# Row sums of a gated graph network, placed chunk by chunk among the other products of a step

## The chip, the cores and the metric

One Trainium2 chip, one core. The metric is the device time of one execution in microseconds; smaller is better. The kernel before ran in 6172.09 us (median of 3 runs, 6161.12 to 6196.0).

## The reference

A normalised input goes through a three-layer gated graph network (GGNN) and is added back. There are 12,500 nodes with 128 features, and 212,500 edges (src, dst), sorted by dst, with a self loop on each node.

```
h = relu(layernorm(x)) @ lin_w.T + lin_b
for i in range(3):
    m   = h @ weight[i]                          # messages, 12500 x 128
    agg = segment_sum(m[src], dst)               # per node, over its edges
    gi, gh = agg @ w_ih.T + b_ih, h @ w_hh.T + b_hh      # 3 gates each
    r, z = sigmoid(ir + hr), sigmoid(iz + hz)
    n    = tanh(in + r * hn)
    h    = (1 - z) * n + z * h
out = x + h
```

All of it is float32. Biases are small random values.

## The kernel before

**Data.** Messages are stored in DRAM as three bf16 pieces per row (384 values, 768 bytes) whose sum is the float32 value. Edges are handled in quads: 4 chunks (`QC`) of 128 edges. There are 416 quads, grouped in 13 superblocks of 32. Since edges are sorted by destination, the sums of one quad fall in a window of 36 nodes (`W`).

**Two ways to sum.** *Gathered quads*: GpSimd (POOL) fetches the 128 message rows of a chunk with one indirect DMA (L458); TensorE (PE) multiplies each of the 3 pieces by a 128 x 36 one-hot matrix of the edges' destinations (L699), 12 products a quad, accumulated in a PSUM window, and VectorE (DVE) adds the window to `aggT` at the quad's node offset (L1009). *Dense quads*, in layers 1 and 2 alone: the first 12 (`DQ`) quads of each superblock are replaced by a matrix of counts (source node x destination within the window), so that the sum is counts times all messages, which lie on chip (`pieces_region`). One dense block is 128 source nodes: 3 products of 128 x 432 (L730), accumulated over 98 blocks for each superblock in PSUM bank 6 or 7, then 12 adds on DVE (L1023).

**Layer 0** gathers all 416 quads and beside it makes the counts for layers 1 and 2: 156 dense quads x 7 rounds = 1092 counting rounds. DVE makes the one-hots of a round (4 instructions, L1089; every seventh round also 4 of L1078), PE multiplies them (4 products of 128 x 504, L712) into PSUM bank 6 or 7 alternately, ScalarE (ACT) copies the bank out (L581), and after seven rounds SP stores the counts (L405).

**Steps.** A step is two gathered quads: 8 gathers, 24 row products. Layer 0 has 208 steps, layers 1 and 2 have 130 each. `rounds_by(s)` and `blocks_by(s)` say how many rounds or dense blocks are to be done before step s: mostly six rounds a step (in steps 6 to 195), mostly ten dense blocks (30 products). A fixed table `TILES_AT` puts the update of each of 49 tiles of 256 nodes behind the step after which its sums are complete.

**Order on PE before.** Step s: wait for the rows, the one-hots of the step and the add of two steps ago; the 24 row products in one run, the last of which signals `s_sum`; the tile update if there is one (4 records for the messages of the tile before, 6 for the state, 6 for the gates; each float32 product leaves two records); then the step's rounds or dense blocks. Each round waits for its one-hots (`s_x`) and for ACT's copy of two rounds ago (`s_ev`).

**Who waits for the sum.** The gathered rows lie in a ring of four step slots (`RING`). POOL, before the gathers of step n, waits until PE has summed step n - 4 (`s_sum`). DVE's step s: add the sums of s (wait for `s_sum`), make half of the round one-hots of step s + 1, the tile update's part, the one-hots of the gathered rows of step s + 2 (L986), the other half of the round one-hots. ACT's step s: copy out half of the step's rounds, its part of the tile update (activations, table loads, stores of the state and the messages, the load of the next state tile), then the other half.

Of the kernel before, what the change touches and what calls it, by code (L numbers as in the profile page):

```python
# [5 lines left out]
P = 128  # L6
# [43 lines left out]
def gated_graph_layers(nc, x, src, dst, lin_wT, lin_b, weight, w_ihT, w_hhT, b_ih, b_hh, out, messages, states, counts):  # L50
# [75 lines left out]
    with ExitStack() as ctx:  # L126
# [192 lines left out]
        def window(n, q):  # L319
            return psum[:, 4 + n % 2, q * W:(q + 1) * W]  # L320
# [149 lines left out]
        def _(act):  # L470
# [117 lines left out]
            for s, n in each_step(0):  # L588
                r0, r2 = rounds_by(s), rounds_by(s + 1)
                r1_ = (r0 + r2) // 2  # L590
                for r in range(r0, r1_):
                    evacuate(r)
                for t in TILES_AT[0].get(s, ()):
                    with act.If(late < 1):
                        tile_update(0, t)
                    act.end_ifs()
                for r in range(r1_, r2):
                    evacuate(r)
            with act.If(late < 1):
# [15 lines left out]
        def _(pe):  # L615
# [74 lines left out]

            def sum_step(layer, s, n):
                pe.wait_ge(s_oh, n + 1)
                if n >= 2:
                    pe.wait_ge(s_add, 2 * (n - 1))
                pe.wait_ge(s_rows[n % RING], 16 * 2 * QC * (n // RING + 1))
                for h in range(2):
                    for c in range(QC):
                        for k in range(PIECES):
                            mm = nc.tensor.matmul(window(n, h), rows[:, n % RING, h * QC + c, k * P:(k + 1) * P],  # L699
                                                  onehot[:, n % 3, h * QC + c, :], start=(c == 0 and k == 0),  # L700
                                                  stop=(c == QC - 1 and k == PIECES - 1))
                mm.then_inc(s_sum, 1)

# [70 lines left out]
            for layer in range(LAYERS):  # L774
                extra_windows(layer)
                for s, n in each_step(layer):
                    sum_step(layer, s, n)
                    for t in TILES_AT[layer].get(s, ()):
                        with pe.If(late < 1):
                            tile_update(layer, t, s)  # L780
                        pe.end_ifs()
                    if layer == 0:
                        for r in range(rounds_by(s), rounds_by(s + 1)):
                            count_round(r)
                    else:
                        for d in range(blocks_by(s), blocks_by(s + 1)):
                            dense_block(layer, d)
                with pe.If(late < 1):
# [401 lines left out]
```

## Time and profile before

| | |
|---|---|
| median of 3 runs | 6172.09 us |
| profiled execution | 6174.11 us |
| its span | 6171.7 us |
| mean granted TensorE clock | 0.785 |
| instructions | 75641 |
| layer 0, 208 steps | 145 to 2853 us |
| layer 1, 130 steps | 2884 to 4506 us |
| layer 2, 130 steps | 4547 to 6149 us |

The span is from the first to the last instruction. PE is TensorE's products and PEld its weight loads, which run beside the products. A wait is put down to what released it; "issue" means that the profile shows nothing that the engine waited for, "remote" that the event that released it isn't in the records.

### The profile page before, as it was taken

To read this page: it belongs to the slowest core of one execution; us is meant where nothing else is said; L and a number is where in the kernel's file an instruction comes from. 1 tells how busy PE (TensorE), PEld (TensorE's weight loads), DVE (VectorE), ACT (ScalarE), POOL (GpSimd) and SP (SyncE) were. 2 spreads that over 40 slices of the span, in tenths; PEclk is the share of its full clock that TensorE was granted. 3 is DMA by queue.
4 is the path that set the end of the run, shared out by engine and by line. 5 is a ranking of instruction groups with operands and counts; after the bars stand their busy time and mean duration, and the time that the engine had idled before them with its cause. 6 is when DMAs were issued, how large, how long until landed. Compare 5 with 4: busy or idle time off the path is not lost.

```text
span 6171.7 us, 75641 instructions
## 1 busy us (share of the span) xinstructions
PE 3893.6 (63%) x25848; PEld 2077.0 (34%) x25849; DVE 2624.7 (43%) x11328; ACT 1090.7 (18%) x2007; POOL 4054.7 (66%) x3806
## 2 busy tenths in 40 slices
PE   4455655566555664652777777776647677677766
PEld 3222222222222222321344444343323344344433
DVE  6566766677675775841122222222211222222222
ACT  3233333333332332321000000010000000000000
POOL 5777777777777776775666666665636666666664
PEclk7677877787787787875888888888768888888888
DMA  6444444444444443454555555555545555555554
GB/s 207 130 125 123 129 125 123 127 131 124 126 126 115 132 129 106 139 160 111 172 176 163 165 177 169 170 177 166 164 148 169 166 176 172 168 170 166 170 162 117
DMA packets 662858, 921.28 MB, mean 149 GB/s; under 512 B 77112, under 2 KB 549304, under 8 KB 662456
## 3 DMA queue, kind: packets, MB, share of 16 engines
q1 hardware_dynamic: 394152, 483.63, 24.2%
q0 software_dynamic: 179712, 368.29, 21.9%
q10 hardware_dynamic: 88592, 64.25, 3.4%
q8 instruction: 221, 3.62, 0.2%
q14 instruction: 181, 1.48, 0.1%
HBM read 717.82 MB, written 198.05 MB: 148 GB/s over the span
## 4 chain that ended last, share of the span: by engine, by line
PE 33%; another core or an unknown queue 22%; issue 18%; DVE 14%; POOL 6%; ACT 3%; DMA 3%; DVEq 1%; ACTq 0%; POOLq 0%; SPq 0%
PE psum L730 16%; DVE pieces_region L1089 7%; PE psum L712 6%; POOL ring_region L458 6%; PE psum L699 3%; PE psum L688 3%; DVE onehot L986 3%; DMA temps<-states 2%; ACT pieces_region L581 1%; PE psum L659 1%; PE psum L661 1%; PE psum L660 1%; DVE aggT L1009 1%; DVEq L976 1%
## 5 line engine op out<-in xcount | busy, mean ns | idle before, releaser
L458 POOL DMA_INDIRECT ring_region<-messages,edge_src x3744 | 3994.1, 1067 | 2006.9 <-issue 1102.7
L712 PE MATMUL psum<-pieces_region,stage_region 128*128 128x504 bf16 x4368 | 1220.2, 432 | 928.6 <-issue 444.9
L730 PE MATMUL psum<-stage_region,pieces_region 128*128 128x432 f16 x7644 | 1648.5, 370 | 189.5 <-issue 188.3
L1009 DVE TENSOR_TENSOR aggT<-aggT,psum 128x36 f32 x936 | 178.8, 191 | 2611.7 <-remote 1994.6
L1089 DVE TENSOR_SCALAR pieces_region<-iota_round,stage_region 128x504 bf16<-128x504 f16 x4368 | 1281.5, 364 | 16.0 <-issue 15.0
L730 PEld LDWEIGHTS psum<-stage_region,pieces_region 128*128 128x128 bf16 x7644 | 761.8, 102 | 1009.1 <-issue 484.6
L699 PE MATMUL psum<-onehot,ring_region 128*128 128x36 bf16 x11232 | 476.4, 182 | 915.9 <-issue 688.6
L712 PEld LDWEIGHTS psum<-pieces_region,stage_region 128*128 128x128 bf16 x4368 | 416.9, 106 | 1633.2 <-issue 1146.9
L581 ACT CAST pieces_region<-psum 128x504 f16<-128x504 f32 x1092 | 621.5, 580 | 1733.5 <-remote 835.7
L699 PEld LDWEIGHTS psum<-onehot,ring_region 128*128 128x128 bf16 x11232 | 411.7, 99 | 1072.3 <-issue 984.8
L986 DVE TENSOR_SCALAR onehot<-iota_block,edge_rel 128x36 bf16<-128x36 bf16 x3744 | 570.5, 254 | 2.0 <-issue 1.9
L518 ACT ACTIVATE temps<-psum,small 128x256 f32<-128x256 f32 x147 | 69.8, 475 | 1813.0 <-DVE temps L1036 677.7
L688 PE MATMUL psum<-aggT,wih 128*128 128x256 f32 x882 | 270.5, 447 | 56.6 <-DVE aggT L1023 34.5
L540 ACT CAST pieces_out<-psum 128x256 bf16<-128x256 f32 x98 | 36.5, 372 | 1298.2 <-remote 911.9
L688 PEld LDWEIGHTS psum<-aggT,wih 128*128 128x128 f32 x882 | 203.0, 233 | 112.4 <-issue 75.0
L1049 DVE SCALAR_TENSOR_TENSOR temps<-psum,small,temps 128x256 f32<-128x256 f32 x147 | 71.0, 483 | 270.9 <-ACT temps L518 119.2
L1030 DVE TENSOR_TENSOR temps<-psum,pieces_out 128x256 f32<-128x256 f32 x98 | 41.3, 422 | 312.7 <-ACT pieces_out L540 201.0
L659 PE MATMUL psum<-temps,whh 128*128 128x256 f32 x294 | 116.8, 481 | 76.4 <-issue 43.3
L1023 DVE TENSOR_TENSOR aggT<-aggT,psum 128x36 f32 x312 | 60.3, 193 | 196.9 <-remote 87.8
L1078 DVE TENSOR_SCALAR stage_region<-iota_block,stage_region 128x128 bf16<-128x128 bf16 x624 | 121.7, 268 | 9.9 <-remote 7.8
L661 PE MATMUL psum<-temps,whh 128*128 128x256 f32 x294 | 114.3, 475 | 6.0 <-issue 5.8
L660 PE MATMUL psum<-temps,whh 128*128 128x256 f32 x294 | 113.7, 472 | 5.2 <-issue 4.8
(84 smaller groups left out, 1393.2 us busy)
## 6 DMA issues: line engine op xcount, KB each, us to landing
stage_region<-counts SPq DMA_DIRECT2D x364, 768.0 KB
counts<-pieces_region SPq DMA_DIRECT2D x156, 896.0 KB
ring_region<-messages,edge_src POOLq DMA_INDIRECT x3744
pieces_region<-messages SPq DMA_DIRECT2D x21, 1344.0 KB
temps<-states ACTq DMA_DIRECT2D x147, 128.0 KB
messages<-pieces_out ACTq DMA_DIRECT2D x98, 192.0 KB
states<-temps ACTq DMA_DIRECT2D x98, 128.0 KB
messages<-ring_region SPq DMA_DIRECT2D x25, 384.0 KB, 2.8
```

Source lines behind the costliest of these rows:

```text
L458: nc.gpsimd.indirect_dma_start(out=rows[:, n % RING, h * QC + c, :], out_offset=None, in_=messages[layer], in_offset=bass.IndirectOffsetOn ...
L581: nc.scalar.copy(ev[j % 2][:, 2 * i:2 * i + 2, 0:HB * W], psum[:, 6 + r % 2, 0:RW].rearrange("p (s w) -> p s w", w=HB * W)).then_inc(s_ev, 1)
L659: nc.tensor.matmul(GATE_R, whh[:, 0:P], state, start=True, stop=True)
L660: nc.tensor.matmul(GATE_Z, whh[:, P:2 * P], state, start=True, stop=True)
L661: nc.tensor.matmul(GATE_HN, whh[:, 2 * P:3 * P], state, start=True, stop=True).then_inc(s_hn, 1)
L688: nc.tensor.matmul(bank, wih[:, gate * P:(gate + 1) * P], nodes, start=alone, stop=True, skip_group_check=not alone).then_inc(s_gate, 1)
L699: mm = nc.tensor.matmul(window(n, h), rows[:, n % RING, h * QC + c, k * P:(k + 1) * P], onehot[:, n % 3, h * QC + c, :], start=(c == 0 and ...
L712: mm = nc.tensor.matmul(psum[:, 6 + r % 2, 0:RW], blocks_oh[j % 2][:, c, :], xs[r % XSLOTS][:, c, :], start=(c == 0), stop=(c == QC - 1))
L730: mm = nc.tensor.matmul(psum[:, 6 + kg % 2, 0:DQ * W], res[:, b, piece * P:(piece + 1) * P], stage[v % ABUF][:, :, cols], start=(b == 0 an ...
L986: made = nc.vector.tensor_scalar(onehot[:, n % 3, h * QC + c, :], iota_lo[:, 0:W], edge_rel[:, q * QC + c:q * QC + c + 1], None, ALU.is_equal)
L1009: nc.vector.tensor_tensor(cols, cols, window(n, h), ALU.add).then_inc(s_add, 1)
L1089: made = nc.vector.tensor_scalar(xs[r % XSLOTS][:, c, :], iota_hi[:], keys[:, j * QC + c:j * QC + c + 1], -float(RW * i), ALU.subtract, AL ...
```

## The change

On PE, a step's 24 row products are cut into eight chunks of three (one for each gathered chunk of 128 rows). After chunk i come the rounds, in layers 1 and 2 the dense blocks, from i/8 to (i + 1)/8 of the step's number. The last chunk signals `s_sum`; with six rounds, the last of them comes after it, with ten blocks the last two. The tile update follows the step's rounds or blocks, where it stood between the row products and them. ACT copies out all of a step's rounds ahead of its part of the tile update. Nothing changes on DVE, POOL and SP, and the number of instructions stays.

```diff
@@ ACT, layer 0
             for s, n in each_step(0):
-                r0, r2 = rounds_by(s), rounds_by(s + 1)
-                r1_ = (r0 + r2) // 2
-                for r in range(r0, r1_):
+                for r in range(rounds_by(s), rounds_by(s + 1)):
                     evacuate(r)
                 for t in TILES_AT[0].get(s, ()):
                     with act.If(late < 1):
                         tile_update(0, t)
                     act.end_ifs()
-                for r in range(r1_, r2):
-                    evacuate(r)
@@ PE
-            def sum_step(layer, s, n):
+            def rows_ready(n):
                 pe.wait_ge(s_oh, n + 1)
                 if n >= 2:
                     pe.wait_ge(s_add, 2 * (n - 1))
                 pe.wait_ge(s_rows[n % RING], 16 * 2 * QC * (n // RING + 1))
-                for h in range(2):
-                    for c in range(QC):
-                        for k in range(PIECES):
-                            mm = nc.tensor.matmul(window(n, h), rows[:, n % RING, h * QC + c, k * P:(k + 1) * P],
-                                                  onehot[:, n % 3, h * QC + c, :], start=(c == 0 and k == 0),
-                                                  stop=(c == QC - 1 and k == PIECES - 1))
-                mm.then_inc(s_sum, 1)
+
+            def sum_chunk(n, i):
+                h, c = i // QC, i % QC
+                for k in range(PIECES):
+                    mm = nc.tensor.matmul(window(n, h), rows[:, n % RING, i, k * P:(k + 1) * P],
+                                          onehot[:, n % 3, i, :], start=(c == 0 and k == 0),
+                                          stop=(c == QC - 1 and k == PIECES - 1))
+                if i == 2 * QC - 1:
+                    mm.then_inc(s_sum, 1)
@@ PE, the steps
                 for s, n in each_step(layer):
-                    sum_step(layer, s, n)
+                    rows_ready(n)
+                    if layer == 0:
+                        first, last = rounds_by(s), rounds_by(s + 1)
+                    else:
+                        first, last = blocks_by(s), blocks_by(s + 1)
+                    for i in range(2 * QC):
+                        sum_chunk(n, i)
+                        for j in range(first + (last - first) * i // (2 * QC),
+                                       first + (last - first) * (i + 1) // (2 * QC)):
+                            if layer == 0:
+                                count_round(j)
+                            else:
+                                dense_block(layer, j)
                     for t in TILES_AT[layer].get(s, ()):
                         with pe.If(late < 1):
                             tile_update(layer, t, s)
                         pe.end_ifs()
-                    if layer == 0:
-                        for r in range(rounds_by(s), rounds_by(s + 1)):
-                            count_round(r)
-                    else:
-                        for d in range(blocks_by(s), blocks_by(s + 1)):
-                            dense_block(layer, d)
```

## Rows read from the trace of the kernel before

**Rows 1.** The page, part 1: busy us, share of the span, instructions.

```profile
PE 3893.6 (63%) x25848; PEld 2077.0 (34%) x25849; DVE 2624.7 (43%) x11328; ACT 1090.7 (18%) x2007; POOL 4054.7 (66%) x3806
```

**Rows 2.** Windows, by layer: busy (records) of PE, PEld, DVE, ACT, POOL; granted clock; DMA.

```profile
145.00:2853.00 2708.00, 1523.80 (x10124) 723.15 (x10124) 1781.93 (x7384) 850.05 (x1469) 2000.36 (x1652) 0.75 0.46 129
2884.00:4506.00 1622.00, 1148.36 (x7690) 651.02 (x7690) 362.33 (x1762) 108.23 (x279) 982.54 (x1031) 0.81 0.55 170
4547.00:6149.00 1602.00, 1123.31 (x7598) 632.28 (x7598) 346.37 (x1717) 65.39 (x141) 979.80 (x1032) 0.82 0.52 163
```

**Rows 3.** Waits in layer 0: who, for whom, us in total, times, longest.

```profile
POOL ring_region L458 <- PE psum L699: 133.2, 21, 16.9
POOL ring_region L458 <- remote: 78.3, 23, 6.2
```

**Rows 4.** Waits in layer 1.

```profile
PEld psum L699 <- issue: 321.8, 293, 19.8
...
PEld psum L730 <- issue: 265.4, 564, 2.7
POOL ring_region L458 <- remote: 160.5, 58, 5.0
POOL ring_region L458 <- PE psum L699: 146.5, 40, 9.6
...
PE psum L699 <- DMA ring_region<-messages,edge_src: 20.8, 2, 19.6
...
PE psum L688 <- DVE aggT L1023: 14.9, 6, 4.1
```

**Rows 5.** Waits in layer 2.

```profile
POOL ring_region L458 <- remote: 182.2, 67, 4.1
POOL ring_region L458 <- PE psum L699: 116.6, 32, 7.1
```

**Rows 6.** Timeline, layer 1: start us, us, instruction, times [idle before].

```profile
4414.35 0.76 PE L699 MATMUL psum<-onehot,ring_region 128*128 128x36 bf16 x24
...
4414.57 1.20 DVE L986 TENSOR_SCALAR onehot<-iota_block,edge_rel 128x36 bf16<-128x36 bf16 x8
...
4414.96 5.64 PE L730 MATMUL psum<-stage_region,pieces_region 128*128 128x432 f16 x30
...
4416.06 0.94 POOL L458 DMA_INDIRECT ring_region<-messages,edge_src  x1 [0.30 <-issue]
...
4420.43 0.51 PE L699 MATMUL psum<-onehot,ring_region 128*128 128x36 bf16 x14
...
4430.51 1.25 PE L730 MATMUL psum<-stage_region,pieces_region 128*128 128x432 f16 x3 [1.59 <-issue]
```

**Rows 7.** Timeline, layer 0, a step with a tile update.

```profile
1116.20 1.46 PE L688 MATMUL psum<-aggT,wih 128*128 128x256 f32 x6
...
1119.80 2.78 PE L712 MATMUL psum<-pieces_region,stage_region 128*128 128x504 bf16 x12 [0.44 <-ACT pieces_region L581]
...
1120.11 0.50 DVE L1009 TENSOR_TENSOR aggT<-aggT,psum 128x36 f32 x2
...
1120.81 3.62 DVE L1089 TENSOR_SCALAR pieces_region<-iota_round,stage_region 128x504 bf16<-128x504 f16 x12 [0.20 <-PE psum L712]
...
1126.90 1.28 ACT L581 ACT_TABLE_LOAD   x1 [0.45 <-issue]
...
1128.92 1.84 PE L712 MATMUL psum<-pieces_region,stage_region 128*128 128x504 bf16 x4 [6.34 <-ACT pieces_region L581]
```

**Rows 8.** Timeline, layer 0, a sum whose signal comes late.

```profile
1410.01 0.93 PE L699 MATMUL psum<-onehot,ring_region 128*128 128x36 bf16 x24
...
1429.89 0.52 DVE L1009 TENSOR_TENSOR aggT<-aggT,psum 128x36 f32 x2 [20.76 <-remote]
...
1430.58 1.84 PE L712 MATMUL psum<-pieces_region,stage_region 128*128 128x504 bf16 x4 [16.16 <-ACT pieces_region L581]
...
1437.40 4.55 PE L712 MATMUL psum<-pieces_region,stage_region 128*128 128x504 bf16 x20
```

## The prediction

> **What bounds the kernel now.** I read the page first, then the table of windows by stage, the waits of each stage, and three short timelines.
>
> The page [rows 1] shows no engine near full: POOL 66%, PE 63%, DVE 43%. Such shares are averages over stages with different limits, so I cut the span at the layers [rows 2]. Layer 0 runs from 145 to 2853 us: 208 steps in 2708 us, 13.0 us a step. Layers 1 and 2 have 130 steps each, in 1622 and 1602 us, 12.5 and 12.3 us a step. The remaining 240 us are prologue, layer ends and the last tile; the change doesn't touch them.
>
> POOL first. A gather is 0.95 us and the 0.30 us after it [rows 6], so eight are 10.0 us. In layer 0 the records of POOL average 2000/1652 = 1.21 us [rows 2], 1.51 us with the 0.30: eight are 12.1 us. What POOL waits for beyond that is a ring slot, that is, PE's row sum of four steps ago: 133.2 + 78.3 = 211 us in layer 0 [rows 3], 146.5 + 160.5 = 307 us in layer 1 [rows 4], 116.6 + 182.2 = 299 us in layer 2 [rows 5] ("remote" has a missing semaphore record; the instruction waits for the same thing). Check: 208 x 12.1 + 211 = 2730 against 2708; 130 x 10.0 + 307 = 1607 against 1622. So layer 0 is set by POOL for 92% of its time, with PE late now and then; in layers 1 and 2 POOL is held up by PE in about 98 steps of 130.
>
> PE in layers 1 and 2. A step that runs freely takes 0.76 us for the 24 row products and 5.64 us for 30 dense ones [rows 6], 6.4 us, half of the 12.4. Yet the PE isn't waiting for rows (20.8 us in all of layer 1 [rows 4]). From 4420.4 on the same timeline shows why it is slow: 14 row products go at full speed, then the rest of that sum and the dense products after it come a few at a time, with idle gaps such as the 1.59 us ahead of three dense products at 4430.5, inside one accumulation, where the program has no wait. The waits put these gaps down to "issue": on the weight loads 321.8 us at the row products and 265.4 us at the dense ones in layer 1 [rows 4]. What holds instructions back I can't see, but their count fits: 2 x 7690/1622 = 9.48 loads and products per us in layer 1, 2 x 7598/1602 = 9.49 in layer 2, 2 x 10124/2708 = 7.5 in layer 0 [rows 2]. Two stretches with the same rate to 0.1%, made of quick 6.4 us steps and slow stretches, look like a limit on how many instructions PE gets through over time, not on array time.
>
> **The change part by part.** No instruction is added or removed, and the gathers, DMAs and evacuations are the same number. What moves is where the row sum ends, where the tile update stands, and ACT's order.
>
> 1. Layers 1 and 2, the sum's end. Each of the 8 chunks (3 products) is followed by an eighth of the step's 30 dense products. The sum, and so the signal that frees the ring slot and lets DVE add, now ends after 7/8 of the dense work: 0.875 x 5.64 = 4.9 us later at full clock. Behind it on POOL are that step's eight gathers. Does the PE then lack rows? A POOL that waits for a slot has three later steps already issued; three steps are at least 3 x 6.4 = 19 us of PE work, and the new gathers need 10.0 us plus their landing. With 4.9 us more, 19 - 10 - 4.9 leaves 4 us for it in the worst case, against 37 us at the average step. Cost 0; if the cover goes, up to 4.9 us at each of some 100 waiting steps a layer, 490 us a layer. That is the end above; I take 0, since the nearest row is the 20.8 us that PE waits for rows in layer 1 now. On DVE the one-hots of step n+2 are made behind the add of step n: add 0.50 [rows 7] and one-hots 1.20 [rows 6], needed a whole step (6.4 us) later. Hidden.
>
> 2. Layers 1 and 2, PE's time. Same instructions, same dense products; if the limit is their number per us, 0. This is my value. The end above it is the 606 us that POOL waits in both layers (the first rival); the end below is part 1's.
>
> 3. Layers 1 and 2, the tile update now comes behind the step's dense work. From one tile update to the next there is one step of dense work and one row sum, before and after. 0; the sums it needs are older then, which could give back a little of the 14.9 us that it waits for DVE's adds [rows 4].
>
> 4. Layer 0, the ring. The sum used to end 0.8 us into the step; now five of the (mostly) six counting rounds come before its last chunk. A round of 4 products is 4.55/5 = 0.91 us at the 2.4 GHz level and 1.84 us at 1.2 GHz [rows 8]: 4.6 to 9.2 us later. POOL waits 44 times in layer 0 [rows 3]. At each the slot now comes 4.6 to 9.2 us later, 202 to 405 us if nothing is given back. But a wait arises after PE was held up, mostly in the rounds, and PE then has three steps of rows to catch up on, so lost POOL time comes back in part where the next wait is shorter. I take a quarter of the middle, (202 + 405)/2/4 = 76 us; bounds 0 and 405.
>
> 5. Layer 0, DVE and PE in a ring of two. DVE makes the count one-hots of step s+1 after its add of step s. Before, the add needed only the quick sum; now it needs five rounds of the same step, which need DVE's previous step. So the shortest period is DVE's add, five rounds of one-hots, the gather one-hots, and then PE's last needed round, chunk and signal: 0.50 + 5 x 1.21 (a round: 3.62/3 [rows 7]) + 1.20 = 7.8, plus 0.91 to 1.84 for the round and some 0.6 us, an estimate, for the signal: 9.3 to 10.2 us. That is below POOL's 12.1, so in plain steps it costs nothing.
>
> In the 45 steps of layer 0 that have rounds and a tile update it isn't hidden. Today [rows 7]: adds at 1120.11, and the next ones only behind the sum that follows the round at 1128.92, so near 1132, 12 us later. PE does the tile products by 1117.7, five rounds by 1122.6, and then idles 6.34 us for ACT, which is in the tile update until 1126.9 and loads a table until 1128.2. After: the step began near 1117.7 - 3.9 (16 tile products at 1.46/6 = 0.24 us) - 0.8 = 1113.0. Sum and five rounds then end at 1113.0 + 0.8 + 5 x 1.0 = 1118.8 and the add starts near 1119.4; the last round and the tile products follow until 1123.7. PE's 6.34 us of idle goes. What is late next: ACT's part, which today takes some 7.7 us from its third copy (near 1120.5, the products are in the row of 1119.80) to 1128.2. The same from 1121 to 1123.7, when the gates come, ends at 1128.7 to 1131.4; DVE's part ends with it, less the table load of 1.28. Behind it stand the gather one-hots 1.2 and the fourth and fifth round 2.4, which the next step's sum now needs, and PE's round, chunk and signal 1.6: the next add comes at 1132.6 to 1135.3, 13.2 to 15.9 us behind the last one instead of 12. A plain step after it gives some 2 us back against POOL's 12.1. I take 1 us a tile step, 45 us; bounds -60 (some of the idle is gained) and 3.9 x 45 = 176, and 0.91 x 190 = 173 us more if the round that now lies between DVE's works shows in each of the 190 steps with rounds.
>
> 6. ACT's merged order and SP's stores of counts: each store waits for seven evacuations in a row that PE gates; they move by at most the half step and nothing waits for them but the second buffer after them. 0.
>
> The signal of a sum can be much later than its products: the products at 1410.01 are done in 0.93 us, DVE adds only at 1429.89, after 20.76 us of idle [rows 8]. The Trainium skill ("TensorE: Matmul & The Clock Gate", its table and "Back-to-back issue gap") has an instruction queue 64 deep on TensorE; the rows fit work that is queued and retired late, though none shows the queue. In the changed order such a delay would stand in DVE's loop too; that is in the upper end of part 5.
>
> **The sum.** Against the profiled execution, 6174.1 us around a span of 6171.7 (median of the runs 6172.1): 6174 + 76 + 45 - 15 (part 3) = 6280 us.
>
> **The rivals.** *Faster: the gaps come from the bursts.* In the timeline the slow stretch begins inside the 24 row products, which leave the queue at 0.76/24 = 32 ns each, against 188 ns for a dense one [rows 6]. If running out of fetched instructions there starts each slow stretch, spreading the burst prevents it, and POOL sets all layers: up to 606 us of its waits go, 5568 us. For it: the place where the gaps start. Against it: the equal rates in both layers, and gaps that go on through dense products. I price it at a quarter of the waits, 6174 - 150 = 6025.
> *No change:* PE's delay is absorbed, since POOL still sets layer 0 and instruction count layers 1 and 2: 6174. For it, POOL's 92%; against it, POOL's waits in layer 0 already today.
> *Much slower: the DVE-PE loop sets layer 0.* It decides if its period, 9.3 to 10.2 us plus the delayed signals, passes POOL's 12.1. At 14.5 us a step: 208 x 1.5 = 312, 6486 us.
> *The clock.* PE has 0.75 of full clock in layer 0, 0.81 and 0.82 after [rows 2]; a mean of 0.81 between the levels 0.5 and 1 means 38% of the time at 1.2 GHz. If spreading keeps it at 2.4 GHz, rounds gain 0.9 us each, but POOL's 12.1 us hides that: part of the second rival, or at best 1% in layer 0's waits.
> PE fell to 1.84 us a round after 16.16 us of idle and did 0.91 us rounds from 1437.4 on [rows 8]. The same page of the Trainium skill ("HAM oscillation") advises running products that belong together before the next wait, or the clock is lost; by it a change that puts the rounds' waits inside the sum goes towards "much slower", whose price from rows stands above. The trace agrees as far as the slow rounds after an idle stretch go.
>
> **How the numbers follow.** Forecast 0.46 (its own range 6215 to 6370), faster 0.22, no change 0.22, much slower 0.10. About 0.5%, 31 us, is what a measurement tells from no change. Faster by more than that 0.24 (the rival and an edge of "no change"), within 0.22, slower 0.54. For 8 in 10 the range reaches into both rivals: 6080 to 6450.
>
> **What would show it.** Layers 1 and 2 keep 12.3 to 12.5 us a step and 9.5 loads and products per us; layer 0 grows from 2708 to some 2820, with POOL's waits for PE well above 211 us and DVE's wait before the add longer. Wrong: if layers 1 and 2 shrink towards 10 us a step (the first rival); if layer 0 stays at 13.0 (parts 4 and 5 hidden); if PE waits for rows in layers 1 and 2 (part 1's cover was too thin).

## The result and the profile after

The change costs 0.6%: 6227.45 us (median of 20 runs, 6196.43 to 6252.46) against 6194.09 us for the kernel before beside it (20 runs, 6161.12 to 6233.08). The ratio is 1.0057, 95% interval 1.0038 to 1.0075. The forecast was 6280 us, 106 us above its profiled execution; the measured loss is some 35 us. The direction was right, the size three times too large, and the place wrong, as the profile shows: the direction was luck, since the two delays that the forecast added up in layer 0 came to nothing and the loss stands in a term that it put at 0.

The first part of the page of the changed kernel (busy us, share of the span, instructions):

```profile
PE 3946.1 (63%) x25848; PEld 2122.3 (34%) x25849; DVE 2619.8 (42%) x11328; ACT 1101.1 (18%) x2007; POOL 4058.4 (65%) x3806
```

Every count of instructions is that of [rows 1]. PE is busy 52.5 us longer and POOL 3.7 us. The windows of the changed kernel, one per layer (length, busy us and records of PE, PEld, DVE, ACT, POOL, granted clock, DMA share, GB/s), answer to [rows 2]:

```profile
145.00:2856.00 2711.00, 1528.85 (x10124) 794.26 (x10124) 1774.75 (x7384) 858.97 (x1469) 2010.95 (x1652) 0.81 0.46 128
2888.00:4524.00 1636.00, 1165.37 (x7690) 638.66 (x7689) 364.08 (x1761) 109.31 (x279) 977.76 (x1031) 0.82 0.54 168
4566.00:6194.00 1628.00, 1151.75 (x7595) 617.12 (x7593) 345.67 (x1716) 65.62 (x140) 976.81 (x1031) 0.81 0.52 160
```

The profiled execution took 6219.76 us, 46 us more than that of before. Layer 0, where the forecast put 121 us, went from 2708 to 2711 us, 13.0 us a step as before: the prediction's own sign that parts 4 and 5 are hidden. Layer 1 grew by 14 us and layer 2 by 26 us, and that is the loss. PE's granted clock in layer 0 rose from 0.75 to 0.81, and the layer is no shorter for it.

What POOL waited for in layer 0 of the changed kernel (us in total, times, longest), against [rows 3]:

```profile
POOL ring_region L458 <- PE psum L696: 133.5, 61, 11.9
POOL ring_region L458 <- remote: 78.2, 22, 6.5
```

211.7 us against 211.5, in 83 waits where there were 44. The waits of the changed kernel in layer 1, against [rows 4]:

```profile
PEld psum L728 <- issue: 368.2, 563, 2.7
...
PEld psum L696 <- issue: 295.4, 496, 2.7
...
PE psum L728 <- issue: 224.6, 292, 2.6
...
PE psum L696 <- issue: 192.0, 228, 2.3
POOL ring_region L458 <- PE psum L696: 172.6, 43, 8.6
```

The same view of the kernel before, its two rows for idle time ahead of the products themselves:

```profile
PE psum L699 <- issue: 284.0, 284, 2.7
...
PE psum L730 <- issue: 107.2, 168, 1.9
```

Ahead of the row and dense products, idle time of PE that the profile can't explain is 391 us in layer 1 before and 417 us after, and much of it moved from the row products to the dense ones. Ahead of the tile update's products it fell by as much, from 37 to 12 us. Its two largest rows before, then the largest one after:

```profile
PE psum L659 <- issue: 17.7, 8, 6.0
...
PE psum L672 <- issue: 12.0, 14, 2.5
```

```profile
PE psum L668 <- issue: 3.9, 8, 1.0
```

So PE's idle time doesn't hold the loss: all of it together is 1622 - 1148 = 474 us in layer 1 before and 1636 - 1165 = 471 us after. What grew is PE's busy time, by 17 us in layer 1 and 28 us in layer 2. The records explain how a hold-up can count as busy: each row product is recorded with 0.18 us (below), but in a run they overlap, so that 24 of them take 0.76 us. Standing apart they cover more time: the row products of layer 1 are busy for 147 us before and 271 us after, at the same number. I therefore count distances from the start of one PE product to the start of the next, leave out those where the second waited for something that the profile names, and call a distance of over 0.5 us held back. In layers 1 and 2 (e1 to e8 and f1 are runs described below):

| kernel | held back in layer 1, in layer 2 | time of these distances, both layers |
|---|---|---|
| before | 485, 493 | 1143 us |
| old order, ring of three (e6) | 479, 482 | 1099 us |
| changed | 531, 551 | 1228 us |
| changed, again (e5) | 543, 529 | 1218 us |
| changed, ring of three (e7) | 518, 536 | 1216 us |
| parts of the change on other chips (e1, f1) | 1 to 3 each | 2 us |

The three profiles of the new order have 1054 to 1082 such distances, the two of the old order 961 and 978. In the changed kernel they take 85 us more than before. The shorter distances behind row products take 25 us more too. About 70 us come back, at the tile update's products (347 to 303 us) and where a product waited for a cause that the profile names (91 to 64 us). What is left is the 40 us of the two layers.

The gaps themselves can be seen in the timeline of the changed kernel, layer 1, engine PE (start, length, instruction, times, idle before), where a free stretch ends and a held-back one begins:

```profile
4414.89 0.23 PE L696 MATMUL psum<-onehot,ring_region 128*128 128x36 bf16 x3
4414.97 0.71 PE L728 MATMUL psum<-stage_region,pieces_region 128*128 128x432 f16 x3
4415.51 0.36 PE L696 MATMUL psum<-onehot,ring_region 128*128 128x36 bf16 x3
4415.72 0.71 PE L728 MATMUL psum<-stage_region,pieces_region 128*128 128x432 f16 x3
4417.11 0.71 PE L728 MATMUL psum<-stage_region,pieces_region 128*128 128x432 f16 x3 [0.69 <-issue]
4417.85 0.18 PE L696 MATMUL psum<-onehot,ring_region 128*128 128x36 bf16 x1
4419.29 0.18 PE L696 MATMUL psum<-onehot,ring_region 128*128 128x36 bf16 x1 [1.26 <-issue]
```

Until 4416 a chunk and its share of dense products take 0.6 us. Then single products of one chunk, between which the program has no wait, stand 1.4 us apart. Cutting the burst of row products hasn't ended such stretches; there are more held-back products than before.

### The profile page after: what moved, and what is told of

Read it like the earlier page. It is cut to its first block, busy times and chain, and to the rows that moved or that the text cites. A ratio compares the mean times of both kernels' runs of the same rounds, so it can differ in the third digit from the quotient of the medians.

```text
span 6217.3 us, 75641 instructions
## 1 busy us (share of the span) xinstructions
PE 3946.1 (63%) x25848; PEld 2122.3 (34%) x25849; DVE 2619.8 (42%) x11328; ACT 1101.1 (18%) x2007; POOL 4058.4 (65%) x3806
## 4 chain that ended last, share of the span: by engine, by line
PE 38%; issue 21%; another core or an unknown queue 16%; DVE 12%; POOL 8%; ACT 2%; DMA 2%; DVEq 1%; ACTq 0%; POOLq 0%; SPq 0%
PE psum L728 21%; POOL ring_region L458 8%; PE psum L710 7%; DVE pieces_region L1093 6%; PE psum L696 3%; PE psum L684 2%; DVE onehot L990 2%; DMA temps<-states 1%; PE psum L655 1%; DVE aggT L1013 1%; PE psum L656 1%; PE psum L657 1%; DVE stage_region L1082 1%; ACT pieces_region L581 1%
## 5 line engine op out<-in xcount | busy, mean ns | idle before, releaser
L728 PE MATMUL psum<-stage_region,pieces_region 128*128 128x432 f16 x7644 | 1901.4, 381 | 453.8 <-issue 452.0
L710 PE MATMUL psum<-pieces_region,stage_region 128*128 128x504 bf16 x4368 | 1276.7, 425 | 915.1 <-issue 356.1
L696 PE MATMUL psum<-onehot,ring_region 128*128 128x36 bf16 x11232 | 866.4, 183 | 729.4 <-issue 485.3
L696 PEld LDWEIGHTS psum<-onehot,ring_region 128*128 128x128 bf16 x11232 | 799.3, 102 | 1520.8 <-issue 1017.0
L728 PEld LDWEIGHTS psum<-stage_region,pieces_region 128*128 128x128 bf16 x7644 | 631.8, 101 | 979.0 <-issue 743.9
L710 PEld LDWEIGHTS psum<-pieces_region,stage_region 128*128 128x128 bf16 x4368 | 368.8, 104 | 1306.3 <-issue 757.6
L518 ACT ACTIVATE temps<-psum,small 128x256 f32<-128x256 f32 x147 | 69.6, 474 | 1891.2 <-remote 1037.7
L684 PE MATMUL psum<-aggT,wih 128*128 128x256 f32 x882 | 236.2, 405 | 25.8 <-DVE aggT L1027 16.3
L684 PEld LDWEIGHTS psum<-aggT,wih 128*128 128x128 f32 x882 | 181.3, 207 | 62.0 <-issue 34.0
L655 PE MATMUL psum<-temps,whh 128*128 128x256 f32 x294 | 106.5, 443 | 52.3 <-DMA temps<-states 28.4
L656 PE MATMUL psum<-temps,whh 128*128 128x256 f32 x294 | 101.6, 430 | 4.0 <-issue 4.0
L657 PE MATMUL psum<-temps,whh 128*128 128x256 f32 x294 | 99.2, 421 | 2.9 <-issue 2.8
L520 ACT ACTIVATE temps<-psum,small 128x256 f32<-128x256 f32 x147 | 69.4, 472 | 103.2 <-remote 49.1
```

The costliest lines, as they stand in the source:

```text
L655: nc.tensor.matmul(GATE_R, whh[:, 0:P], state, start=True, stop=True)
L656: nc.tensor.matmul(GATE_Z, whh[:, P:2 * P], state, start=True, stop=True)
L684: nc.tensor.matmul(bank, wih[:, gate * P:(gate + 1) * P], nodes, start=alone, stop=True, skip_group_check=not alone).then_inc(s_gate, 1)
L696: mm = nc.tensor.matmul(window(n, h), rows[:, n % RING, i, k * P:(k + 1) * P], onehot[:, n % 3, i, :], start=(c == 0 and k == 0), stop=(c ...
L710: mm = nc.tensor.matmul(psum[:, 6 + r % 2, 0:RW], blocks_oh[j % 2][:, c, :], xs[r % XSLOTS][:, c, :], start=(c == 0), stop=(c == QC - 1))
L728: mm = nc.tensor.matmul(psum[:, 6 + kg % 2, 0:DQ * W], res[:, b, piece * P:(piece + 1) * P], stage[v % ABUF][:, :, cols], start=(b == 0 an ...
```

## Experiments

One thing must be known to read the numbers. The kernel before took about 6190 us in the runs of the result above and on the chip of e5 to e8, and about 5380 us on four other chips (e1 to e4, f, g and h, with 5385, 5373, 5383 and 5378 us). Each experiment is compared with the kernel before on its own chip. I say "slower kind" and "faster kind" of chip below; whether the difference belongs to the chip itself or to its condition in that hour no run shows. Several expectations name the other kind of chip than the one that the run then got; what that means for each is said beside its result.

**e5: the change as it is.** No edit.

> The whole change, unaltered, on the chip where the kernel before takes 5385 us and PE has no unexplained gaps. Theory E (the 0.6% were lost in layers 1 and 2 because PE, not POOL, set them there; here POOL issues its gathers without waiting and sets every layer): within 0.3% of before, as its parts were. Rival F (the parts are harmless alone and cost something together, or the loss is in a place that does not depend on PE's gaps): slower by 0.4 to 0.7%.

6230.79 us against 6190.81, ratio 1.0048 (1.0022 to 1.0073). Windows of its three layers:

```profile
146.00:2849.00 2703.00, 1540.07 (x10119) 796.60 (x10116) 1773.73 (x7384) 856.84 (x1468) 1998.69 (x1652) 0.81 0.45 129
2882.00:4525.00 1643.00, 1170.27 (x7687) 639.80 (x7685) 363.56 (x1761) 109.15 (x278) 977.67 (x1031) 0.82 0.54 167
4566.00:6180.00 1614.00, 1153.00 (x7598) 620.52 (x7598) 344.84 (x1716) 66.04 (x141) 978.06 (x1031) 0.81 0.52 162
```

The place of the loss repeats: layer 0 is 5 us shorter than in the first profile of the kernel before, layers 1 and 2 are 21 and 12 us longer. The expectation was written for a chip of the faster kind, so neither of its theories was put to the test: the whole change never ran on one.

**e6 and e7: a ring of three step slots**, in the old and in the new order. If the later end of the sum costs time through the ring, it costs more with a smaller one.

```diff
-RING = 4
+RING = 3
+RING_SPACE = 4
...
```

`RING_SPACE` keeps the memory of the ring at its old size, so that only the number of slots changes.

> The old order with a ring of three step slots in place of four. Theory E: where POOL sets the pace and PE works a step as soon as its rows are in, a slot is free again some 3 us after its rows land, so three slots are enough in layers 1 and 2 (10.0 us a step stays); layer 0 loses where PE is late after a tile update, 50 to 150 us, 1 to 3%. Rival G (the ring is what binds): layers 1 and 2 slower too, by over 1 us a step, 300 us in all.

> The changed order with a ring of three. The predicted cost of the change (each slot held 4.6 to 9.2 us longer in layer 0, 4.9 us in layers 1 and 2) must show here if it shows anywhere, since one slot of cover is gone: slower than the old order with three slots by 50 us or more in layer 0. Rival: the later signal is covered with three slots as well, within 0.3% of the old order with three.

e6: 6192.26 us, ratio 1.0004 (0.9975 to 1.0032). e7: 6243.07 us, 1.0077 (1.005 to 1.0103), so 0.7% over e6. Windows of e6 (old order), then of e7 (new order):

```profile
146.00:2895.00 2749.00, 1552.52 (x10112) 729.71 (x10110) 1782.20 (x7386) 849.25 (x1470) 1956.44 (x1651) 0.75 0.44 127
2926.00:4539.00 1613.00, 1144.56 (x7690) 645.46 (x7690) 359.59 (x1761) 106.97 (x278) 978.64 (x1031) 0.81 0.54 171
4578.00:6174.00 1596.00, 1135.47 (x7593) 635.92 (x7594) 345.28 (x1716) 64.19 (x140) 977.09 (x1031) 0.82 0.52 163
```

```profile
146.00:2900.00 2754.00, 1565.82 (x10119) 800.51 (x10115) 1781.68 (x7386) 861.03 (x1471) 1963.54 (x1652) 0.79 0.44 126
2932.00:4558.00 1626.00, 1159.26 (x7687) 636.79 (x7685) 364.46 (x1762) 109.28 (x279) 978.83 (x1031) 0.82 0.54 169
4597.00:6204.00 1607.00, 1139.95 (x7598) 616.16 (x7597) 345.86 (x1716) 65.75 (x140) 978.67 (x1031) 0.82 0.52 162
```

With one slot fewer, the new order costs 5 us in layer 0, 13 in layer 1 and 11 in layer 2 in these profiles, no more than with four slots. The medians are 51 us apart, against 33 and 40 us with four slots, which the noise of some 0.4% doesn't tell apart. e7's expectation, 50 us or more in layer 0, failed, and so did its rival of 0.3% in all: the loss is there, but in layers 1 and 2. The ring doesn't carry it. e6 missed too: 50 to 150 us were expected in all, and the medians differ by 1.4 us. In one profile each, layer 0 is 41 us longer (2749 against 2708 us) and layers 1 and 2 are 15 us shorter.

**e8: fewer steps, more dense work**, in the old order: 14 instead of 12 dense quads a superblock, so 117 steps instead of 130 in layers 1 and 2, dense products of 504 columns, 1274 counting rounds instead of 1092. To make room, three count buffers instead of four.

```diff
-DQ = 12
+DQ = 14
-ABUF = 4
+ABUF = 3
...
```

> The old order with 14 instead of 12 dense quads in each superblock (dense products of 504 columns, three buffers of counts instead of four): nine steps of gathers a superblock in place of ten in layers 1 and 2, and 1274 counting rounds in layer 0 in place of 1092. Theory E (POOL sets layers 1 and 2 at 10.0 us a step): 26 steps fewer, 260 us less, against up to 100 us more in layer 0: 5180 to 5280 us, 2 to 4% faster. Rival: layer 0 becomes DVE's (its 12.2 us a step grow by a sixth of 6.7 us) and takes most of it back: 5350 or more.

6001.49 us, ratio 0.9674 (0.9641 to 0.9706). Its windows:

```profile
146.00:3001.00 2855.00, 1681.27 (x10852) 775.65 (x10852) 1998.31 (x8216) 955.49 (x1650) 2066.26 (x1652) 0.77 0.46 130
3033.00:4506.00 1473.00, 1154.77 (x7378) 614.38 (x7378) 347.40 (x1658) 107.89 (x279) 881.59 (x927) 0.87 0.61 196
4546.00:5998.00 1452.00, 1141.67 (x7282) 601.42 (x7278) 330.59 (x1612) 65.98 (x141) 880.28 (x927) 0.88 0.59 189
```

Layer 0 pays 147 us for the added counts, layers 1 and 2 give back 299 us. The rate of loads and products is 2 x 7378/1473 = 10.02 per us in layer 1 and 2 x 7282/1452 = 10.03 in layer 2, above the 9.5 that step 2 of the prediction took for a limit on instructions. What stayed is the time of a step: 1473/117 = 12.6 us and 1452/117 = 12.4 us, as before. The held-back time of a step didn't stay: by the count of the section before it is 573 distances and 685 us, 2.9 us a step against 1143/260 = 4.4 us. PE's added work of a step went into time in which it was held back. So neither PE's instructions nor its held-back time was the same for each step in the two kernels, only the sum of work and hold-up, some 12.5 us. A fixed time for a step (eight gathers, a tile update in some) would fit; the runs don't show what would set it. The expected 5180 to 5280 us were for a chip of the faster kind, the 2 to 4% came, and layer 0 lost 147 us where at most 100 were expected.

**e1 and f4: only layer 0 in the new order**; layers 1 and 2 do the row products in one run, then the tile update, then the dense blocks.

```diff
+                    spread = layer == 0
                     for i in range(2 * QC):
                         sum_chunk(n, i)
-                        for j in range(...):
+                        if spread:
+                            for j in range(...):
...
+                    if not spread:
+                        for j in range(first, last):
+                            count_round(j) if layer == 0 else dense_block(layer, j)
```

> The new order in layer 0 alone (with ACT's merged order), the old one in layers 1 and 2. Theory A (the loss is in layers 1 and 2, where the profiled changed kernel took 15 and 28 us more, and POOL still sets layer 0): no change, within 0.3% of before. Rival B (the ring slot and the loop of DVE and PE cost time in layer 0, and the profiled execution happened to show none of it): slower by 0.5% or more, 30 us and up, as much as the full change.

> The new order in layer 0 alone, where PE has the gaps. Theory A: within 0.2% of before; layer 0 takes 2700 to 2715 us, its steps with a tile update shorter, the steps behind them longer by as much. Rival B: slower by 0.3% or more.

e1: 5377.73 us, ratio 0.9988 (0.9973 to 1.0004). f4: 5374.55 us, 0.9998 (0.9981 to 1.0015). No cost. That is theory A's number, but these chips have no held-back stretches, and the other half of theory A fails on them, as the next runs show.

**e2, f1, g1 and h1: only layers 1 and 2 in the new order**: the same edit with `spread = layer > 0`, and ACT's order in layer 0 as before.

> The new order in layers 1 and 2 alone, the old one in layer 0. Theory A: slower by about as much as the full change, 25 to 45 us (0.4 to 0.7%), most of it in steps with a tile update. Rival B: within 0.2% of before.

> The new order in layers 1 and 2 alone, repeated where the kernel before takes some 6190 us and PE has the unexplained gaps (on the other chip, at 5385 us, it had none, and nothing of the change cost time). Theory A (the 0.5% are lost in layers 1 and 2): slower by 0.4 to 0.7%. Rival B (in layer 0, or only together): within 0.2%.

> The new order in layers 1 and 2 alone. If PE has the gaps here: theory A 0.4 to 0.7% slower, rival B within 0.2%. If not: no change, as twice before.

> The new order in layers 1 and 2 alone. If PE has the gaps here: theory A 0.4 to 0.7% slower, rival B within 0.2%. If not: no change, as three times before.

5382.15 us (ratio 0.999, 0.9971 to 1.001), 5377.66 us (1.0008, 0.9993 to 1.0024), 5376.2 us (0.9993, 0.997 to 1.0016) and 5379.71 us (1.0008, 0.999 to 1.0027). No cost on any of the four chips. Theory A's 0.4 to 0.7% missed in e2 and f1, rival B's "within 0.2%" came, and neither is decided for the slower kind, where the loss was measured.

The windows of e1 (layer 0 new, layers 1 and 2 old), then of f1 (layer 0 old, layers 1 and 2 new):

```profile
145.00:2682.00 2537.00, 1553.46 (x10117) 764.64 (x10118) 1776.18 (x7398) 869.83 (x1474) 2028.89 (x1652) 0.80 0.49 137
2710.00:4012.00 1302.00, 1045.29 (x7684) 617.83 (x7685) 370.09 (x1773) 110.83 (x280) 978.22 (x1031) 0.89 0.67 211
4052.00:5350.00 1298.00, 1033.76 (x7599) 604.51 (x7600) 351.31 (x1719) 68.27 (x141) 978.77 (x1031) 0.89 0.65 201
```

```profile
146.00:2673.00 2527.00, 1536.97 (x10125) 763.02 (x10121) 1786.78 (x7398) 858.66 (x1474) 2019.04 (x1652) 0.79 0.48 138
2701.00:4003.00 1302.00, 1043.11 (x7686) 606.37 (x7687) 366.80 (x1761) 109.80 (x277) 979.62 (x1031) 0.90 0.67 211
4045.00:5342.00 1297.00, 1032.31 (x7596) 591.24 (x7595) 349.14 (x1719) 68.32 (x141) 977.64 (x1031) 0.90 0.64 201
```

Layer 1 takes 1302 us in either order, 10.0 us a step: the eight gathers of 1.25 us. What POOL waited for in layer 0, first in e1 (new order), then in f1 (old order):

```profile
POOL ring_region L458 <- PE psum L696: 3.7, 12, 0.3
```

```profile
POOL ring_region L458 <- PE psum L700: 0.9, 3, 0.3
```

3.7 and 0.9 us, where the kernels have 211 us on a chip of the slower kind. And what PE waited for in layer 1 of f1:

```profile
PE psum L700 <- DMA ring_region<-messages,edge_src: 229.5, 87, 6.3
```

Here PE waits for gathered rows (20.8 us in [rows 4]): POOL sets every layer, and the place of PE's work within a step cost nothing measurable.

**e3, f2 and g2: the tile update moved, the sum left in one run**: the row products, all rounds or blocks, then the tile update, in all layers.

```diff
                     for i in range(2 * QC):
                         sum_chunk(n, i)
-                        for j in range(...):
...
+                    for j in range(first, last):
+                        count_round(j) if layer == 0 else dense_block(layer, j)
                     for t in TILES_AT[layer].get(s, ()):
```

> All layers: the 24 row products stay in one run at the start of the step, and the tile update stands behind the rounds or dense blocks, as in the change (ACT's order merged with it). Theory A1 (the loss is the later end of the sums: POOL and DVE get their signal some 5 us later, and the first tile update after it): no loss here, 6170 to 6195. Theory A2 (the loss is the tile update's later place, which lengthens the steps that have one): the whole loss of the change, 0.4 to 0.7%. In layer 0 both expect about 2710 us.

> The row products in one run, the tile update behind the rounds or dense blocks in all layers, where PE has the gaps. Theory A1 (the loss is the spreading, with its later sum): within 0.2% of before. Theory A2 (the loss is the tile update's later place): slower by 0.4 to 0.7%.

> The row products in one run, the tile update behind the rounds or dense blocks. If PE has the gaps here: theory A1 (the spreading costs) within 0.2%, theory A2 (the tile update's place costs) 0.4 to 0.7% slower. If not: no change.

5386.65 us (ratio 1.0005, 0.999 to 1.0019), 5378.34 us (1.0003, 0.9984 to 1.0022) and 5390.45 us (1.0012, 0.9988 to 1.0035). No cost, which on these chips tells nothing between A1 and A2: the spreading alone costs nothing on them either.

**e4, f3, g3 and h2: more PE instructions for the same work**, in the old order. Each dense product of 432 columns becomes two of 216 with the same weights loaded twice.

```diff
-mm = nc.tensor.matmul(psum[:, 6 + kg % 2, 0:DQ * W], ...)
+for part in range(2):
+    mm = nc.tensor.matmul(psum[:, 6 + kg % 2, part * DQ // 2 * W:(part + 1) * DQ // 2 * W], ...)
```

> The old order; each dense product of 432 columns in layers 1 and 2 is made as two of 216 columns with the same weights loaded twice, so 30 more loads and 30 more products a step for the same columns. Theory C (PE is held to about 9.5 loads and products per us over time, so layers 1 and 2 go by their number): 12.4 us a step becomes (118 + 60)/9.5 = 18.7 us, layers 1 and 2 together 1600 us longer, 7800 us in all. Rival D (columns and the clock set PE's time, and the gaps come from the burst of row products): at the 2.4 GHz level 60 products of 216 columns are as long as 30 of 432, so under 0.5 us a step more, 130 us or less in all.

> Each dense product of layers 1 and 2 as two of 216 columns, 30 more loads and products a step for the same columns, where PE has the gaps. Theory C (what holds PE there goes by the number of its instructions): 12.4 us a step becomes 15 to 19 us, 700 to 1600 us longer in all. Rival D (it goes by something else: columns, the clock, time): under 100 us. On the other chip the same kernel took 0.1% more at 17.9 instructions per us, so a limit of 9.5 cannot be in PE itself.

> Each dense product of layers 1 and 2 as two of 216 columns. If PE has the gaps here: theory C (they go by the number of instructions) 700 to 1600 us longer; rival D under 100 us. If not: no change, as twice before.

> Each dense product of layers 1 and 2 as two of 216 columns. If PE has the gaps here: theory C (they go by the number of instructions) 700 to 1600 us longer; rival D under 100 us. If not: no change, as three times before.

5393.58 us (ratio 1.0013, 0.9998 to 1.0028), 5377.24 us (1.0005, 0.9989 to 1.0022), 5383.08 us (1.0001, 0.9979 to 1.0023) and 5383.88 us (1.0014, 0.9995 to 1.0033). The windows of layers 1 and 2 of e4:

```profile
2733.00:4036.00 1303.00, 1047.30 (x11512) 976.75 (x11512) 367.79 (x1763) 110.71 (x280) 979.66 (x1031) 0.90 0.67 211
4076.00:5375.00 1299.00, 1038.64 (x11422) 965.03 (x11423) 350.44 (x1720) 68.03 (x141) 979.59 (x1031) 0.90 0.65 201
```

2 x 11512/1303 = 17.7 loads and products per us (the expectation of f3 has 17.9), at most 8 us or 0.15% over the kernel before: 9.5 is no limit of PE on this kind of chip. Theory C's 700 to 1600 us didn't come, but they were expected where PE is held back, and none of the four runs was there. Against such a limit on the slower kind stands e8 alone. Two timeline rows of e4, layer 1:

```profile
3505.86 0.76 PE L699 MATMUL psum<-onehot,ring_region 128*128 128x36 bf16 x24 [0.70 <-DMA ring_region<-messages,edge_src]
3506.46 5.71 PE L731 MATMUL psum<-stage_region,pieces_region 128*128 128x216 f16 x60
```

60 products of 216 columns take 5.71 us where 30 of 432 take 5.64 [rows 6]. A chip of the faster kind doesn't run a free step quicker; it lacks the held-back stretches.

**g4: 14 dense quads and the new order together**, the edit of e8 on the changed kernel.

> The changed order with 14 dense quads a superblock and three buffers of counts. If PE has the gaps here: 0.3 to 0.8% slower than the old order with 14, which was 0.967 of before, so 0.970 to 0.975. If not: POOL sets layers 1 and 2 and 26 steps of 10.0 us go, against a longer layer 0: 0.95 to 0.98.

5235.6 us, ratio 0.9722 (0.9684 to 0.9759) to the kernel before on its chip. The windows of layers 1 and 2:

```profile
2831.00:4011.00 1180.00, 1063.83 (x7372) 573.98 (x7373) 351.46 (x1656) 109.79 (x277) 882.43 (x927) 0.97 0.75 245
4047.00:5215.00 1168.00, 1060.10 (x7287) 562.82 (x7285) 335.58 (x1615) 68.25 (x141) 880.52 (x927) 0.96 0.73 235
```

1180/117 = 10.1 us a step, again the gathers; the expected 0.95 to 0.98 came. On both kinds of chip a kernel with 14 dense quads beats the kernel before by some 3%, the old order on the slower kind and the new order on the faster one: layers 1 and 2 have 26 steps fewer at the same time a step. What the order is worth at 14 wasn't measured, since no chip ran both orders with 14.

## Why the prediction was wrong in size

**Part 4, the ring in layer 0 (+76 us): this step failed.** It is worth 0 (211.5 us of waits before, 211.7 after, 140.6 + 73.7 = 214 in e5). The prediction charged each of the 44 waits with the later signal and gave three quarters back; all of it came back. My reading is that the sum ends later within its step while PE isn't late by the step, and that a wait arises where PE is held back for longer than the ring covers. On the chips that don't hold it back, POOL's waits in layer 0 are 0.9 us (f1, old order) and 3.7 us (e1, new order). So the waits go with the held-back stretches and not with where in the step the sum ends. A thinner ring changes that little: POOL's waits in layer 0 are 236.0 + 55.6 = 292 us in e6 and 248.8 + 60.2 = 309 us in e7, and the layer is 5 us longer.

**Part 5, the loop of DVE and PE (+45 us): this step failed too, in its sum and in part of its local account.** The prediction said that in a tile step the 6.34 us of idle goes, and that the next add comes 13.2 to 15.9 us behind the last one. DVE's adds of the changed kernel around that tile step:

```profile
1110.86 0.52 DVE L1013 TENSOR_TENSOR aggT<-aggT,psum 128x36 f32 x2 [0.24 <-PE psum L696]
1118.79 0.52 DVE L1013 TENSOR_TENSOR aggT<-aggT,psum 128x36 f32 x2 [0.24 <-PE psum L696]
1127.70 0.52 DVE L1013 TENSOR_TENSOR aggT<-aggT,psum 128x36 f32 x2 [0.24 <-PE psum L696]
1143.99 0.52 DVE L1013 TENSOR_TENSOR aggT<-aggT,psum 128x36 f32 x2 [3.79 <-PE psum L696]
```

The step after the tile took 16.3 us, a little over the range. The idle time didn't all go; in that step PE stands idle for 3.64 us, and the round behind it runs at the 1.2 GHz level:

```profile
1137.21 1.83 PE L710 MATMUL psum<-pieces_region,stage_region 128*128 128x504 bf16 x4 [3.64 <-issue]
```

One step also isn't typical. From the add of a step with a tile update to the next add, the 45 steps that have rounds took 21.8 us on average before and 19.1 us after: shorter, where the account had 1 us more. The two steps before the tile took 7.9 us (five rounds, of which the sum needs four) and 8.9 us (six rounds), 3 to 4 us below POOL's 12.1. For six rounds 9.3 to 10.2 us had been worked out as the shortest period, so that part was slightly too long. The account gave some 2 us back and stopped after one step. Counted over the layer from the starts of PE's row products, the 48 steps with a tile update shrank from 22.3 to 14.7 us (-366 us), the 47 behind them grew from 10.2 to 17.2 (+330), and the other 112 grew by 0.35 (+40): a transfer between neighbours that ends near zero. That it does so because four ring slots and POOL's 12.1 us lie between it and the layer's end is my reading, not a thing that a run separates. The 173 us held ready for a round that shows in each step didn't come either.

**Parts 1 to 3, layers 1 and 2 (0, 0 and -15 us): here is the loss, so part 2's 0 is the term that was too small.** The loss is 14 and 26 us in the profiled execution, 21 and 12 in e5, 13 and 11 from e6 to e7. Part 1's cover held: POOL's waits for PE went from 307 to 331 us in layer 1, but PE isn't short of rows: it waits 20.8 us for them in all of layer 1, as in [rows 4]. Part 2 took the rate of 9.5 loads and products per us for a limit on instructions, and so valued a reordering at 0. e8 contradicts that reason (10.0 per us on such a chip), and e4 has 17.7 on the other kind. The rate in the changed kernel is 2 x 7690/1636 = 9.40 and 2 x 7595/1628 = 9.33. What grew is the number of held-back products, from 978 to 1082 in both layers, and their time by 85 us, of which about half was given back elsewhere. Part 3's own text takes 0, yet the sum subtracts 15 us for it; without them the forecast would be 6295 us. Of these 15 us, 3.3 us can be found in layer 1, where PE's wait for DVE's adds ahead of the gates went from 14.9 us [rows 4] to 11.6. Steps with and without a tile update share the loss differently in the two profiles of the changed kernel, so they don't say which edit it belongs to.

**The rivals.** *Faster, the gaps come from the bursts* fell: the gaps go on without bursts, inside chunks of three. *No change* named the right reason for layer 0. *Much slower* didn't come: the periods of plain steps, such as the 7.9 and 8.9 us above, stayed below POOL's 12.1 us. *The clock* went as that rival had it: 0.75 to 0.81 in layer 0, hidden behind POOL. Added up from the clock's records, PE stood at 1.2 GHz for some 1350 us of layer 0 before and 1050 after. A round that waits for its one-hots inside the sum of the changed kernel, layer 0:

```profile
1116.52 1.02 PE L710 MATMUL psum<-pieces_region,stage_region 128*128 128x504 bf16 x4 [1.06 <-DVE pieces_region L1093]
```

After 1.06 us of idle it runs at 0.26 us a product, the 2.4 GHz level; the round behind 6.34 us of idle took 1.84 us [rows 7]. The Trainium skill ("TensorE: Matmul & The Clock Gate", "HAM oscillation") warns that waits between groups of products lose the clock; its case is one of long DMA waits. The trace agrees for long idle, the 6.34 us before and the 3.64 us above. With many waits of about 1 us in place of some long ones the mean clock rose here, against the direction that I took from the page.

**What stays open.** Which part of the change costs the 0.5%, the spreading or the tile update's place: the experiments that separate them ran on chips that don't hold PE back, where neither costs anything. The same for what holds PE back on the slower kind. Ruled out are a fixed rate of 9.5 PE instructions per us (e8) and a burst as the only trigger (the timeline after); a constant time per step or per gather fits e8, but it was seen in one kernel alone. Nor do the runs show why the new order has some 10% more held-back products. That the loss needs the held-back stretches is shown only so far as it is there in all three comparisons with them (the result, e5, and e7 against e6) and absent, within 0.4%, part by part on the four without; the whole change wasn't run on one of those.

## What to carry to other kernels

Where one engine sets a stage (here POOL with 12.1 us a step) and a ring of several slots lies between, moving another engine's work within the step was a transfer between neighbouring steps: add up whole steps until the ring is passed before charging a delay, and don't multiply a local delay by the number of waits. A rate that two stages share isn't a limit until a kernel with another mix keeps it; a change of the mix (14 dense quads) is both the test and, here, the gain of 3%. Idle time alone can hide a hold-up, since a product that stands alone is recorded as busy for longer: count distances from start to start as well. Time a kernel on more than one chip before optimising idle time that the profile can't explain.

## What the runs showed of the hardware

The same program took 6190 us in the runs of the result and of e5 to e8, and 5380 us on four other chips, 15% more on the slower kind, each level steady to about 1%. The free step of PE and the 1.25 us of a gather are the same on both kinds. The difference is PE held back between products that wait for nothing in the program: 978 distances of over 0.5 us in layers 1 and 2 of the kernel before, against 3 or 4 in e1 and f1, and no more than 7 between 2950 and 5150 us in any profile from the four faster chips. Four in five of the 978 lie within 0.08 us of a multiple of 0.7 us, as the 1.4 us in the timeline of the changed kernel. With it come POOL's waits for PE: 211 and 307 us in layers 0 and 1 on one kind, 4 us or less in layer 0 on the other. On the faster kind the granted clock in layers 1 and 2 is 0.89 to 0.90 instead of 0.81 to 0.82. A step of PE, DVE and ACT in a loop with the sum between them ran in 7.9 us with five counting rounds and 8.9 us with six, a little quicker than the chain worked out from single durations for six (9.3 to 10.2 us).
